# L1 attention: joint quarter sums of a moved tile, four score transfers a pair, weights normalised by ScalarE

## The reference

```
v = (x @ wqv_w.T + wqv_b).reshape(b, t, 3 * h, d);  q, vf, vb = its thirds
k = x[:, :, None, :] * wk[None, None]
a[b, s, t, h] = -sum_w |q[b, s, h, w] - k[b, t, h, w]| / sqrt(64)
a = softmax over s of (a with one more row of zeros)[:, :t]
bf = einsum('bsdh,bshw->bdhw', a, vf);  bb = einsum('bdsh,bshw->bdhw', a, vb)
o = (bf + bb).sum(heads);  y = o * sigmoid(1.702 * o);  return x + y @ fanin_w.T + fanin_b
```

## Time and profile before

| | us |
|---|---|
| median of 3 runs | 2579.07 (2578.93 to 2579.52) |
| the profiled execution | 2576.05 |
| its span | 2574.2 |
| L1 attention, first to last reduce (L1454) | 721.7 to 2465.7 |

### The profile page before, as it was taken

One profiled execution on the slowest core, in us unless ns is written; L12 is line 12 of the kernel. 1 busy time (PEld: TensorE's weight loads), 2 busy tenths in 40 slices (PEclk: granted clock), 3 DMA queues, 4 the chain that ended last, 5 costly groups with the idle time before them and its releaser, 6 DMA issues.

```text
span 2574.2 us, 45353 instructions
## 1 busy us (share of the span) xinstructions
PE 2236.6 (87%) x12251; PEld 961.1 (37%) x12251; DVE 2244.8 (87%) x2638; ACT 1475.2 (57%) x3772; POOL 1767.2 (69%) x1033
## 2 busy tenths in 40 slices
PE   5558999999388989989989989899899899899878
PEld 3443333333123333333333333333333333333347
DVE  3877777777879999999999999999999999999974
ACT  0325555555146666666666666666666666666656
POOL 0112333333459889888888988888898888889843
PEclk8788999999689999999999999999999999999979
DMA  5200000000012112121211221221221212212201
GB/s 132 65 1 1 1 0 0 0 0 0 3 47 52 48 48 52 48 50 49 51 48 48 52 50 45 51 51 45 50 52 48 50 48 50 50 47 52 50 19 32
DMA packets 163216, 102.06 MB, mean 40 GB/s; under 512 B 55773, under 2 KB 161182, under 8 KB 163039
## 3 DMA queue, kind: packets, MB, share of 16 engines
q1 hardware_dynamic: 162858, 101.41, 16.0%
q10 hardware_dynamic: 316, 0.12, 0.0%
HBM read 10.63 MB, written 4.19 MB: 6 GB/s over the span
## 4 chain that ended last, share of the span: by engine, by line
PE 65%; DVE 23%; issue 9%; ACT 1%; DMA 1%; DVEq 0%; SPq 0%; POOL 0%; ACTq 0%; POOLq 0%
DVE score L1454 17%; PE pp L802 16%; PE pp L796 7%; PE pp L636 5%; PE pp L767 3%; PE pp L657 3%; PE pp L723 3%; PE pp L715 2%; PE pp L661 2%; PE pp L731 2%; PE pp L711 2%; PE pp L721 2%; PE pp L658 2%; PE pp L662 2%; PE pp L628 2%
## 5 line engine op out<-in xcount | busy, mean ns | idle before, releaser
L1454 DVE TENSOR_REDUCE score<-pp 128x16 f32<-128x1024 f32 x1408 | 1647.0, 1219 | 101.9 <-PE pp L802 82.2
L1571 POOL TENSOR_TENSOR absd<-absd 128x2560 f32<-128x2560 f32 x635 | 1442.4, 2271 | 197.1 <-ACT absd L1074 157.2
L802 PE MATMUL pp<-blocks,pick 128*128 128x512 f16 x2816 | 817.0, 383 | 155.0 <-DVE score L1454 150.4
L1074 ACT ACTIVATE absd<-pp 128x512 f32<-128x512 f32 x1280 | 695.4, 598 | 368.0 <-PE pp L796 364.1
L802 PEld LDWEIGHTS pp<-blocks,pick 128*128 128x128 f16 x2816 | 211.2, 98 | 590.7 <-DVE score L1454 421.9
L796 PE MATMUL pp<-blocks,pick 128*128 128x512 f16 x1280 | 400.0, 383 | 2.1
L1538 POOL TENSOR_TENSOR absd<-absd,yw 128x512 f32<-128x512 f32 x112 | 142.1, 1269 | 318.8 <-DVE yw L1376 318.8
L1008 ACT ACTIVATE absd<-pp 128x512 f32<-128x512 f32 x256 | 150.7, 596 | 148.1 <-PE pp L658 146.6
L1392 DVE SCALAR_TENSOR_TENSOR absd<-pp,absd 128x512 f32<-128x512 f32 x256 | 172.5, 688 | 52.9 <-ACT absd L1008 38.4
L796 PEld LDWEIGHTS pp<-blocks,pick 128*128 128x128 f16 x1280 | 119.8, 97 | 248.3 <-ACT absd L1074 84.6
L1056 ACT CAST qk<-pp 128x512 f16<-128x512 f32 x130 | 76.0, 585 | 191.2 <-PE pp L724 191.2
(11 more groups left out here) (227 smaller groups left out, 2497.9 us busy)
## 6 DMA issues: line engine op xcount, KB each, us to landing
blocks<-qk SPq DMA_DIRECT2D x1032, 64.0 KB, 2.0
attn<-score SPq DMA_DIRECT2D x1024, 16.0 KB, 1.8
xs<-xn SPq DMA_DIRECT2D x66, 32.0 KB, 1.8
big<-in_wrb_t SPq DMA_DIRECT2D x1, 2064.0 KB
big<-in_x_rows SPq DMA_DIRECT2D x4, 512.0 KB, 6.1
token_rows<-big SPq DMA_DIRECT2D x8, 256.0 KB, 2.0
big<-in_L_ffn_w SPq DMA_DIRECT2D x4, 512.0 KB, 10.1
out<-h SPq DMA_DIRECT2D x16, 128.0 KB, 2.0
```

The costliest lines, as they stand in the source:

```text
L802: mm = pe.matmul(ps[bank + n], pick[:, unit % 8 + n, :], blocks[:, b, unit // 16, unit // 8 % 2, :], start=True, stop=True)
L1074: nc.scalar.activation(absd[odd][:, 16 * u + 8 * n:16 * u + 8 * n + 8, :], ps[4 + n].rearrange("p (h w) -> p h w", w=D), ACT.Abs).then_inc ...
L1454: dve.tensor_reduce(score[:, odd, b, 16 * d:16 * d + 16], pp[:, bank:bank + 2, :].rearrange("p n (h w) -> p (n h) w", w=D), AX.X, ALU.add, ...
L1571: nc.gpsimd.tensor_tensor(x[:, :, 0:w], x[:, :, 0:w], x[:, :, w:2 * w], ALU.add).then_inc(X["tree"], 1)
```

## The change

1. `ORDER` becomes `"DADDADDADDADADED"`: 10 D steps, 5 A steps, and one E step (k = 14) an image. `NP` is the number of A steps, `NA` = `NP` + 1.
2. The E step computes the last tile with its operands swapped (four matmuls of 256 columns, the tile of `blocks` as stationary operand), so that the widths lie on the rows. ScalarE writes its absolute values to `abse`. In the next pair, behind the D step k = 11 of the first image, `sum_e` sums over the rows for both images together: 8 f32 products with a stationary operand of 32 columns (`pair_ones`), in four strips of 32 output rows. ScalarE copies the result (`copy_e`), `turn_e` turns it with two small products against `row_of` (behind k = 13), and ScalarE puts it into `score` (`take_e`).
3. `pick` has another order of combinations, so that a spread takes one transfer for 128 columns of an image: 4 a pair. The first half of an image's scores is sent once 8 of its D steps are reduced, the second half once everything is there, `take_e` included.
4. `normalise` moves to ScalarE, a head at a time (8 instructions, in two groups of 4 in the first image of a later pair); the exponentials are issued in four groups of 2.
5. `low` no longer repeats the f32 product: it accumulates on what `queries` or `keys` left in bank 6.
6. `turn_attn` stands behind k = 5 instead of 4; `gated` behind the eighth reduce of the second image instead of the ninth. `c_cols` now shares the memory of `absd0`.

```diff
-ORDER = "DADDADDADDADDADD"
-ND, NA = ORDER.count("D"), ORDER.count("A")
+ORDER = "DADDADDADDADADED"
+ND, NP = ORDER.count("D"), ORDER.count("A")
+NA = NP + 1
...
+    row_of = np.zeros((4, 32, 2, 4, 2))
+    for m in range(4):
+        for b in range(2):
+            for a in range(2):
+                row_of[m, 2 * b + a, b, m, a] = 1.0
...
+        absd = [t[:, 0:NP * 1024].rearrange("p (n w) -> p n w", w=D) for t in (absd0, absd1)]
+        abse = [t[:, NP * 1024:NA * 1024].rearrange("p (m n) -> p m n", m=4) for t in (absd0, absd1)]
...
+            def spread(p, odd, b, j, first):
+                if j == 0:
+                    sp.wait_ge(X["red"], ND * (2 * p + b) + 8)
+                else:
+                    sp.wait_ge(X["red"], ND * (2 * p + b + 1))
+                    sp.wait_ge(X["pooled"], 2 * p + b + 1)
+                    sp.wait_ge(X["etaken"], p + 1)
                 if not first:
                     sp.wait_ge(X["exp"], p)
-                for j in range(2):
-                    for x in range(4):
-                        sp.dma_start(attn[64 * b + 32 * j:64 * b + 32 * j + 32, 16 * x:16 * x + 16, :].rearrange("p s h -> p (s h)"),
-                                     score[32 * x:32 * x + 32, odd, b, P * j:P * j + P]).then_inc(X[f"spread{b}"], 16)
+                sp.dma_start(attn[64 * b + 32 * j:64 * b + 32 * j + 32, 0:S, :].rearrange("p s h -> p (s h)"),
+                             score[:, odd, b, P * j:P * j + P]).then_inc(X[f"spread{b}"], 16)
...
             def low(p, odd, kind):
                 pe.wait_ge(X["half"], 4 * p + 2 * kind + 1)
-                if kind:
-                    pe.matmul(ps[6], xT1[:, odd, :], wk_diag[:].rearrange("p h d -> p (h d)"), start=True, stop=False)
-                else:
-                    pe.matmul(ps[6], xTq[:], wqv[:, 0:QK], start=True, stop=False)
-                pe.matmul(ps[6], neg_eye[:], qk[:, kind, 0, :], start=False, stop=True).then_inc(...)
+                pe.matmul(ps[6], neg_eye[:], qk[:, kind, 0, :], start=False, stop=True, skip_group_check=True).then_inc(...)
...
+            def sum_e(p, first):
+                pe.wait_ge(X["abs"], 4 * NA * (p + 1))
+                if not first:
+                    pe.wait_ge(X["etaken"], p)
+                for m in range(4):
+                    for b in range(2):
+                        mm = pe.matmul(ps[7][32 * m:32 * m + 32, 0:2 * P], pair_ones[:, b, :], abse[b][:, m, :],
+                                       start=(b == 0), stop=(b == 1))
+                mm.then_inc(X["e_ps"], 1)
+
+            def turn_e(p):
+                pe.wait_ge(X["esum"], p + 1)
+                for g in range(2):
+                    mm = pe.matmul(ps[7][:, 256 + 16 * g:272 + 16 * g], esum[:, P * g:P * g + P], row_of[:], start=True, stop=True)
+                mm.then_inc(X["et_ps"], 1)
...
+                            if path == "A":
+                                unit = 2 * (ND + u) + n
+                                mm = pe.matmul(ps[4 + n], pick[:, unit % 8, :], blocks[:, b, unit // 16, unit // 8 % 2, :],
+                                               start=True, stop=True)
+                            else:
+                                for m in range(2):
+                                    mm = pe.matmul(ps[4 + n][:, 256 * m:256 * m + 256],
+                                                   blocks[:, b, 1, 1, P * (2 * n + m):P * (2 * n + m) + P],
+                                                   pick[:, 6:8, :].rearrange("p a b -> p (a b)"), start=True, stop=True)
...
+                        if k == 11 and at >= 1:
+                            sum_e(q - 1, at == 1)
+                        if k == 13 and at >= 1:
+                            turn_e(q - 1)
...
-                            if k == 4:
+                            if k == 5:
                                 turn_attn(q - 2)
```

ScalarE's program for a pair afterwards (s counts images, `absolute` with last index 5 is the E step):

```diff
+            def copy_e(p):
+                act.wait_ge(X["e_ps"], p + 1)
+                act.wait_ge(X["et_ps"], p)
+                nc.scalar.copy(esum[:], ps[7][:, 0:2 * P]).then_inc(X["esum"], 1)
+            def take_e(p, odd, at):
+                act.wait_ge(X["et_ps"], p + 1)
...
+                nc.scalar.copy(score[:, odd, :, 240:256].rearrange("p b (g h) -> p g b h", g=2),
+                               ps[7][:, 256:288].rearrange("p (g b h) -> p g b h", g=2, b=2)).then_inc(X["etaken"], 1)
+            def normalise(p, part, first):
...
+                for n in range(4 * part, 4 * part + 4):
+                    op = nc.scalar.activation(attk[:, n, :], expd[:, n, 0:S], ACT.Copy, scale=zst[:, 1, n:n + 1])
...
                 prepare_x(q + 1, 1 - odd)
-                absolute(s, 0, 3, first)
+                if at >= 2:
+                    normalise(q - 2, 0, at == 2)
+                absolute(s, 0, 3, q, first)
                 high_q(q + 1, False)
+                if at >= 1:
+                    copy_e(q - 1)
+                absolute(s, 0, 4, q, first)
                 low(q + 1, 0)
-                absolute(s, 0, 4, first)
+                if at >= 1:
+                    take_e(q - 1, 1 - odd, at - 1)
+                if at >= 2:
+                    normalise(q - 2, 1, at == 2)
+                absolute(s, 0, 5, q, first)
                 s += 1
                 high_k(q + 1)
                 low(q + 1, 1)
...
-                absolute(s, 1, 2, first)
-                absolute(s, 1, 3, first)
+                absolute(s, 1, 2, q, first)
+                if at >= 1:
+                    exponentials(q - 1, 0, at == 1)
+                absolute(s, 1, 3, q, first)
                 if at >= 2:
                     gate_o(q - 2)
                 if at >= 1:
-                    exponentials(q - 1, 0, at == 1)
-                absolute(s, 1, 4, first)
+                    exponentials(q - 1, 1, at == 1)
+                absolute(s, 1, 4, q, first)
                 if at >= 1:
-                    exponentials(q - 1, 1, at == 1)
+                    exponentials(q - 1, 2, at == 1)
+                absolute(s, 1, 5, q, first)
+                if at >= 1:
+                    exponentials(q - 1, 3, at == 1)
```

More of the change, by code:

```diff
@@ L453, in pair @@
                 if at >= 1:
-                    spread(q - 1, 1 - odd, 0, at == 1)
-                    spread(q - 1, 1 - odd, 1, at == 1)
+                    for j in range(2):
+                        for b in range(2):
+                            spread(q - 1, 1 - odd, b, j, at == 1)
                 fill_blocks(q + 1, 0, False)
@@ L466, in _ @@
                     pair(2 * i + odd, odd, 4, bass.ds(2 * i + odd + 2, 1))
-            spread(PAIRS - 1, 1, 0, False)
-            spread(PAIRS - 1, 1, 1, False)
-            sp.wait_ge(X["tb0"], 16 * 8 * (PAIRS + 1))
+            for j in range(2):
+                for b in range(2):
+                    spread(PAIRS - 1, 1, b, j, False)
+            sp.wait_ge(X["tb0"], FILL * (PAIRS + 1))
             sp.wait_ge(X["xs"], 16 * (PAIRS + 2))
@@ L719, in low @@
                 pe.wait_ge(X["half"], 4 * p + 2 * kind + 1)
-                if kind:
-                    pe.matmul(ps[6], xT1[:, odd, :], wk_diag[:].rearrange("p h d -> p (h d)"), start=True, stop=False)
-                else:
-                    pe.matmul(ps[6], xTq[:], wqv[:, 0:QK], start=True, stop=False)
-                pe.matmul(ps[6], neg_eye[:], qk[:, kind, 0, :], start=False, stop=True).then_inc(X["klo_ps" if kind else "qlo_ps"], 1)
+                pe.matmul(ps[6], neg_eye[:], qk[:, kind, 0, :], start=False, stop=True, skip_group_check=True).then_inc(X["klo_ps" if kind else "qlo_ps"], 1)
             def values_b(p, odd, at):
@@ L852, in _ @@
             fan_in(last - 2)
+            pe.wait_ge(X["sum"], last - 1)
+            sum_e(last, False)
+            turn_e(last)
+            pe.wait_ge(X["etaken"], PAIRS)
             def last_turn(p):
@@ L1066, in values_f, with absolute @@
                 nc.scalar.copy(vf[:, odd].rearrange("p i n d -> p (i n d)"), ps[6]).then_inc(X["vf"], 1)
-            def absolute(s, odd, u, first):
+            def absolute(s, odd, u, q, first):
                 for n in range(2):
@@ L1084, in exponentials @@
                         act.wait_ge(X["zr"], p)
-                for n in range(4 * part, 4 * part + 4):
+                for n in range(2 * part, 2 * part + 2):
                     op = nc.scalar.activation(expd[:, n, :], attn[:, :, n], ACT.Exp, scale=-(float(D) ** -0.5),
                                               accum_out=zst[:, 0, n:n + 1])
+                if part == 3:
+                    op.then_inc(X["exp"], 1)
+            def normalise(p, part, first):
+                if part == 0:
+                    act.wait_ge(X["zr"], p + 1)
+                    if not first:
+                        act.wait_ge(X["o_ps"], p)
+                for n in range(4 * part, 4 * part + 4):
+                    op = nc.scalar.activation(attk[:, n, :], expd[:, n, 0:S], ACT.Copy, scale=zst[:, 1, n:n + 1])
```

(20 more changed lines are left out.)

98 lines of the change are left out of this document (53 added, 45 removed).

## The result

The changed kernel takes 2543.59 us (median of 4 runs, 2543.0 to 2544.97) against 2579.07 before: a ratio of 0.9863, 95% interval [0.9846, 0.988], so 1.4% faster, clear of the noise. The forecast was 2611. Its profiled execution has a span of 2541.2 us, 33.0 less than before. The order of this part: what the pair now looks like, then where the 33 us lie.

A forecast was written before the change was run, and what follows sets the result against it. TensorE and VectorE, coupled through two bank pairs, bound the kernel. VectorE's 23.25 us plus 4.50 of stalls make a pair 27.75 against 27.20: +35 over 64 pairs, about 3 saved at the end, so 2611 us, range 2550 to 2660.

The forecast's parts named there:

- What bounds the kernel: L1 attention pairs: TensorE and VectorE coupled, no single engine the bound; 22 reduces 24.9 us, stalls 1.7 of 27.20.
- the walk with two bank pairs: TensorE's order between D steps, followed through two alternating bank pairs: stalls of 4.50 us in the new pair.
- Removed steps and `low`: Per pair, two D steps go, 2.26 us of VectorE and 0.86 of TensorE; `low` loses 0.97 us twice.
- (a): E step on TensorE: four matmuls of 256 columns for two of 512, 0.43 us, up to 0.8.
- (b): `sum_e` on TensorE, behind k = 11 of the first image: 1.98 us by `values_f`, bounds 1.12 and 3.70.
- rival A: `sum_e`'s four strips run side by side in 1.1 us: pair 26.9, whole 2556 us; chance 0.22.
- (c): `turn_e` on TensorE: 4 instructions of 16 columns after f32 weight loads, 0.3 to 0.55 us, taken as 0.45.
- The reciprocal's 0.36: VectorE's reciprocal, counted as 0.36 us of its own work within 0.63 for three small instructions a pair.
- Outside the pairs: End of the stage: fewer spreads save about 3 us, with ScalarE's slower normalisation behind them.
- Rival B: `sum_e`'s order leaves little overlap: 2.4 us, pair 28.2, whole 2639; with none 3.7, 29.5, 2721; chance 0.25.
- Rival C: `sum_e` is 2.0 us but ScalarE does not stand in the way: pair 26.9, whole 2557 us; chance 0.13.
- Rival D: GpSimd becomes the bound with 23.4 us busy; the prediction held that it hides and gave no separate chance.

The follow-up runs named there:

- e1: The changed kernel with `sum_e`'s eight products sent to two strips of 32 output rows in place of four: 2599.66 us.
- e3: The kernel before with one edit of the change alone, `low` no longer repeating the f32 product: 2524.53 us, ratio 0.9788.
- e2: The changed kernel with all eight products of `sum_e` in one strip of 32 output rows: 2707.91 us.
- e12: The changed kernel with `sum_e`'s products reordered, all four strips of the first image, then all four of the second: 2543.51 us, ratio 0.9863.
- e7: The changed kernel with the exponentials in two groups of four, behind k = 7 and E of the second image, not four of two: 2529.46 us.
- e11: The changed kernel with the normalisation put back on GpSimd, one instruction a pair: 2540.01 us, ratio 0.9846.
- e9: The changed kernel without its E step (old `ORDER`), with ScalarE's copy of queries' low half ahead of the absolute values of k = 13: 2530.87 us, ratio 0.9811.
- e10: The changed kernel with exponentials in two groups of four and keys, `sum_e`, `turn_e` and keys' low half moved later: 2535.61 us, ratio 0.9835.
- e5: The changed kernel without its E step and sums (old `ORDER`), the rest of the change kept but for `gated`'s place: 2577.38 us, ratio 0.9992.

## Why the prediction was wrong

- **What bounds the kernel**, and the walk with two bank pairs: right. Every stall of the table but one is within 0.1 us, and with two strips (e1) that one came out too.
- **Removed steps and `low`**: right in size and in place (e3: the stalls of 0.33, 0.24 and 0.22 went with it). I priced `low` only inside the sum, so I did not see that it is the part that pays.
- **(a) E step 0.43**: right. The wait of keys for ScalarE's copy behind it was in the walk as well, with 0.09; it is 0.17, because `turn_e` is as much shorter. What the walk didn't have is that keys take 0.96 behind such a wait, not 0.86.
- **(b) `sum_e` 1.98: this step failed.** I took the price from `values_f`, the nearest row, in which two column halves run at once. It took 1.02, 1.12 with the 0.1 ahead of it, the lower bound and rival A's case (1.1, a stall of 1.07, a pair of 26.9). Worth 0.85 us a pair, 54 us in all. The row of `values_f` has only two column positions; it could not show a third and fourth, and the number of positions was the term to scale by. Rival A's page, the Trainium skill's "TensorEngine Tiling (Array Packing)", Theoretical Speedup, states up to 4x for operands of at most 32 columns, and this case agrees: 3.57 / 1.02 = 3.5 over one strip (e2). The argument against it, from matmuls that stay in program order, gives less overlap for strips issued one behind the other; e12's 1.01 against 1.02 shows no such loss.
- **(c) `turn_e` 0.45**: near enough; 1528.48 to 1528.85 is 0.37, and as keys wait for ScalarE anyway, it changes nothing.
- **The reciprocal's 0.36** was 0.11 of work and 0.25 of stall; in the changed kernel the stall hides behind the 0.55 before it, and e7 brings it back. Worth another 0.25 us a pair, 16 us.
- **Outside the pairs** I had -3 us. It is -10.3 at the half-clock stretches and the start, and +6.1 at the end. The spreads gave their 3 us there (the last lands 3.2 earlier), but the normalisation cost more than the 1 us of its own length: on ScalarE the table load and the layer norm stand behind it (e11: the end is 7.3 us shorter with it on GpSimd).
- **Rival B** (little overlap) fell with the 1.02. **Rival C** (ScalarE out of the way) fell: E waits 0.37 us for it in the second image. **Rival D** fell: GpSimd is in no chain.

By the pair the two mis-sized terms give 27.75 - 0.85 - 0.25 = 26.65, with the 0.10 of keys more at k = 15 the 26.75 measured. What stays open: by what steps the normalisation's move grows to 7.3 us at the end, of which 4.9 are reached at ScalarE's table load; and what decides which pairs meet a stretch at half clock.

## What to carry to other kernels

A product with few output columns should be priced by how many column positions it can fill, not by the nearest row that fills fewer; where the two prices fall on different sides of zero, that is the rival to weigh highest. Walk the order of work through the banks: it gives each stall to a tenth of a microsecond, and it also says that taking one stall away may let out the next. A change of several parts can be faster while its main part costs time; only undoing the parts one by one shows which of them pays. And before an order of work is moved, look up when the hidden transfers land, and what stands ahead of them in their queue: that tells what the move may cost.

## What the runs showed of the hardware

- Eight f32 products of 128x32 by 256 columns (16 instructions) take 1.02 us in four strips of output rows (in either order of issue), 1.88 in two, 3.57 in one.
- Stretches of 3.4 us at half clock (1.2 of 2.4 GHz) inside the stage, 1.6 us each, in the profiled executions: 4 before, 6 with `low` alone (e3), 7 in e9, one in e10, none in the changed kernel and the others. In the row above TensorE was busy for 1.02 of 2.20 us ahead of the fall. All 17 of the first three kernels fall at the same place, within 0.3 us of the start of the third of three steps at the end of a pair that wait 0.40, 0.53 and 0.66 us for reduces, though every pair of theirs has these waits. The kernels with an E step don't have the three. But e5 has them in every pair and has no such stretch, so they are not enough by themselves, and no run here shows what is.
- Keys, two f32 instructions of 512 columns, take 0.96 us where TensorE stood idle until their weight load was released (changed kernel, e5), and 0.86 where it didn't (e3, e9).
